# A four-layer graph network kernel: first-layer normalisation moved between engines, one widening step moved a head earlier, and more filler products at the end of the load

## The reference

```python
h = jnp.maximum(_layernorm(x, axis=-1), 0.0)
x = x + _L0_gnn_ref(h, adj, L0_gnn_weight, L0_gnn_bias)    # D^-1/2 adj^T D^-1/2 (h @ W0) + b0
h = jnp.maximum(_layernorm(x, axis=-1), 0.0)
x = x + _L1_gnn_ref(h, adj)                                # (adj + mask/norm) @ h, over its row sums
h = jnp.maximum(_layernorm(x, axis=-1), 0.0)
x = x + _L2_gnn_ref(h, adj, L2_gnn_W, L2_gnn_a)            # 4 heads of attention, softmax(leaky(s_i+d_j)+adj)
h = jnp.maximum(_layernorm(x, axis=-1), 0.0)
x = x + _L3_gnn_ref(h, adj, L3_gnn_weight)                 # relu(adj @ (binary(h) @ sign(W3)^T))
```

## Time and profile before

| what | value |
|---|---|
| median of 3 runs | 707.07 us (706.51 to 708.0) |
| the profiled execution | 707.33 us, span of its instructions 705.5 us |
| TensorE busy | 684.2 us, 97% of the span |
| VectorE busy | 620.8 us, 88% |
| ScalarE busy | 459.4 us, 65% |
| GpSimd busy | 111.5 us, 16% |
| mean granted TensorE clock | 0.995 |

### The profile page before, as it was taken

One profiled execution on the slowest core, in us unless ns is written; L12 is line 12 of the kernel. 1 busy time (PEld: TensorE's weight loads), 2 busy tenths in 40 slices (PEclk: granted clock), 3 DMA queues, 4 the chain that ended last, 5 costly groups with the idle time before them and its releaser, 6 DMA issues.

```text
span 705.5 us, 15958 instructions
## 1 busy us (share of the span) xinstructions
PE 684.2 (97%) x6413; PEld 584.9 (83%) x6413; DVE 620.8 (88%) x1148; ACT 459.4 (65%) x798; POOL 111.5 (16%) x146
## 2 busy tenths in 40 slices
PE   3989999999999999999999999999999899999998
PEld 3876888888888974488888888888888788888887
DVE  7888999958898968899999999999999799994672
ACT  3987057638888328975559676587866678655650
POOL 3005722321123210011100021100211000000000
PEclk9998999999999999999999999999999999999999
DMA  9996999993799977779988799988999894464391
GB/s 334 378 336 258 424 426 308 303 230 123 219 271 252 208 189 191 192 180 246 214 189 248 143 222 249 232 236 175 203 235 239 222 199 78 83 191 139 130 311 38
DMA packets 169016, 159.53 MB, mean 226 GB/s; under 512 B 115760, under 2 KB 128752, under 8 KB 164720
## 3 DMA queue, kind: packets, MB, share of 16 engines
q1 hardware_dynamic: 147584, 100.32, 52.8%
q0 software_dynamic: 19056, 41.42, 26.2%
q10 hardware_dynamic: 2304, 16.78, 5.7%
HBM read 69.86 MB, written 52.46 MB: 173 GB/s over the span
## 4 chain that ended last, share of the span: by engine, by line
PE 88%; DVE 4%; ACT 4%; issue 3%; POOL 0%; ACTq 0%; POOLq 0%
PE ps L839 16%; PE ps L841 16%; PE ps L840 16%; PE ps L777 6%; PE ps L885 4%; PE ps L886 4%; PE ps L675 3%; PE ps L677 3%; PE ps L676 3%; PE ps L724 3%; PE ps L726 3%; PE ps L725 3%; DVE arena L1253 2%; PE ps L704 2%; DVE arena L1339 1%
## 5 line engine op out<-in xcount | busy, mean ns | idle before, releaser
L839 PE MATMUL ps<-arena 128*128 128x257 f16 x1024 | 279.9, 273 | 1.9 <-DVE arena L1477 1.9
L841 PE MATMUL ps<-arena 128*128 128x257 f16 x1024 | 279.4, 273 | 0.0
L840 PE MATMUL ps<-arena 128*128 128x257 f16 x1024 | 279.2, 273 | 0.0
L1169 ACT ACTIVATE arena<-arena 128x512 f16<-128x512 f32 x252 | 158.4, 628 | 98.0 <-PE ps L841 77.6
L1470 DVE SCALAR_TENSOR_TENSOR arena<-arena,w_j 128x512 f32<-128x512 f32 x256 | 190.0, 743 | 0.0
L1477 DVE TENSOR_TENSOR arena<-arena 128x512 f16<-128x512 f32 x256 | 175.7, 687 | 9.6 <-ACT arena L1169 9.3
L839 PEld LDWEIGHTS ps<-arena 128*128 128x128 f16 x1024 | 99.9, 98 | 14.8 <-ACT arena L1169 2.1
L840 PEld LDWEIGHTS ps<-arena 128*128 128x128 f16 x1024 | 100.3, 98 | 12.6
L841 PEld LDWEIGHTS ps<-arena 128*128 128x128 f16 x1024 | 99.8, 97 | 13.0
L724 PE MATMUL ps<-arena 128*128 128x257 f16 x256 | 70.3, 275 | 0.0
L726 PE MATMUL ps<-arena 128*128 128x257 f16 x256 | 69.7, 272 | 0.0
(11 more groups left out here) (149 smaller groups left out, 1068.0 us busy)
## 6 DMA issues: line engine op xcount, KB each, us to landing
adj_t<-arena POOLq DMA_DIRECT2D x32, 1024.0 KB, 7.9
arena<-in_adj_dram SPq DMA_DIRECT2D x32, 512.0 KB, 6.2
arena<-in_adj_dram SPq DMA_DIRECT2D x16, 1024.0 KB, 6.1
adj_parts<-arena ACTq DMA_DIRECT2D x16, 1024.0 KB, 22.1
arena<-adj_t SPq DMA_DIRECT2D x64, 256.0 KB, 4.9
arena<-adj_t SPq DMA_DIRECT2D x10, 1024.0 KB, 6.7
x<-arena POOLq DMA_DIRECT2D x15, 512.0 KB, 6.2
arena<-u_rows SPq DMA_DIRECT2D x4, 1024.0 KB, 14.7
```

The source lines that it names most:

```text
L839: mm(ps[:, bank, 0:DE], hi, ht_hi[:, head, j, 0:DE], start=s, stop=False)
L840: mm(ps[:, bank, 0:DE], hi, ht_lo[:, head, j, 0:DE], start=False, stop=False)
L841: ins = mm(ps[:, bank, 0:DE], lo, ht_hi[:, head, j, 0:DE], start=False, stop=e)
L1169: nc.scalar.activation(p_hi[:, j % 4, :], prob[:, j % 4, :], copy).then_inc(p_hi_done, 1)
```

## The change

Three things change.

1. The normalised blocks of block 0 go straight into `hw[t]`, each to its own place, instead of into two buffers in turn. VectorE normalises only blocks 0, 4, 8 and 12, at halves 0, 4, 8 and 14 (`NORM_AFTER`). GpSimd normalises the other twelve, three after each of its roots.
2. `WIDEN_AFTER`: block 12 is widened after group 6 (was 7), 13 after 7 (was 8), 14 and 15 after 8 (were 8 and 9).
3. `unread`: three products instead of one per half for n = 24 to 30, and eight instead of six after the last half.

```diff
-        h0_n = view(160 * KB, [2, D], F32)
+        NORM_AFTER = (0, 4, 8, 14)
-        WIDEN_AFTER = {0: (6,), 1: (7,), 3: (8,), 4: (9, 10), 5: (11,), 7: (12,), 8: (13, 14), 9: (15,)}
+        WIDEN_AFTER = {0: (6,), 1: (7,), 3: (8,), 4: (9, 10), 5: (11,), 6: (12,), 7: (13,), 8: (14, 15)}
...
+                pool.wait_ge(rstd_done, p + 1)
+                for t in range(XP * p + 1, XP * p + XP):
+                    nc.gpsimd.tensor_scalar(hw[:, t, :], x[:, t, :], mean_var[:, t, 0:1], rstd[:, t:t + 1],
+                                            ALU.subtract, ALU.mult).then_inc(pool_normed, 1)
...
             def h0_transposes(t):
-                pe.wait_ge(normed, t + 1)
+                if t % XP == 0:
+                    pe.wait_ge(normed, t // XP + 1)
+                else:
+                    pe.wait_ge(pool_normed, t // XP * (XP - 1) + t % XP)
...
-                                              h0_n[:, t % 2, c * P:(c + 1) * P],
+                                              hw[:, t, c * P:(c + 1) * P],
...
-                    unread(1)
+                    unread(1 if n < row_slot(NB - 1) + 2 else 3)
             ins.then_inc(deg_done, 1)
-            unread(6)
+            unread(8)
...
             def h0_norm(t):
-                if t % XP == 0:
-                    dve.wait_ge(rstd_done, t // XP + 1)
-                if t >= 2:
-                    dve.wait_ge(h0_t_ps, t - 1)
-                v.tensor_scalar(h0_n[:, t % 2, :], x[:, t, :], mean_var[:, t, 0:1], rstd[:, t:t + 1],
+                dve.wait_ge(rstd_done, t // XP + 1)
+                v.tensor_scalar(hw[:, t, :], x[:, t, :], mean_var[:, t, 0:1], rstd[:, t:t + 1],
...
-                for t in range(NB):
-                    if row_slot(t) - 1 == n:
-                        h0_norm(t)
+                if n in NORM_AFTER:
+                    h0_norm(XP * NORM_AFTER.index(n))
```

More of the change, by code:

```diff
@@ L254, in gnn_stack @@
         normed = sem("normed")
+        pool_normed = sem("pool_normed")
         h0_t_done = sem("h0_t_done")
```

## The result

| what | before | changed |
|---|---|---|
| median | 707.25 us (706.51 to 708.0, 4 runs) | 713.06 us (711.26 to 714.42, 4 runs) |
| ratio | | 1.0081, 95% interval 1.0056 to 1.0106 |
| the profiled execution | 707.33 us, span 705.5 | 714.42 us, span 712.6 |
| first product of block 0 | 63.73 us | 67.03 us |
| group 0's addition to x (start of block 2's queue) | 329.27 us | 336.36 us |

The changed kernel is 5.8 us slower, where 3 us less was forecast. The traces differ by 7.1 us in span. 3.3 us of it arise in the load, 3.8 us between 67 us and group 0's addition, and nothing net in block 2 and after. A trace is of one execution, and some lie far from the median of their kernel (unread_only's is of 707.89 us, its median 710.52; swap_extra's 710.61 and 706.90; mended's 712.72 and 707.75; tiny_128's 711.84 and 708.09).

A forecast was written before the change was run, and what follows sets the result against it. TensorE, busy 97% of the span, was taken as the bound, leaving only its gaps. Load 1.0, unread products 0.1 and widening 1.86 sum to 2.96 us less: median 704.1 us, 8-in-10 range 702.5 to 706.3.

The forecast's parts named there:

- a GpSimd round is 5.6 us, blocks come in time: Load: a 1.24 us root and three normalisations take 5.6 us, serving four blocks that TensorE takes in about 6 us.
- the hold: Load: time a GpSimd normalisation keeps VectorE from working, taken as 0.3 us, between 0.15 and 0.52.
- No normalisation waits for more than one `adj_low`: Load: GpSimd and VectorE take turns after each instruction, so a normalisation behind one `adj_low` takes 1.45 us in all.
- The third rival: Load: GpSimd holds VectorE 0.9 us per normalisation, rounds last 7.4 us, kernel slower at 709.5 us; chance 0.06.
- the first rival: Load: the hold is an addition's 0.52 us, so the load loses 0.5 us net, kernel at 705.6 us; chance 0.17.
- 2 us less work reach the end with 1.0 us: Load from 35 us to half 24: VectorE has six normalisations less, 2 us; 1.0 us (0.5 to 1.5) shortens the load.
- The clock: Load's tail: the extra unread products keep TensorE's granted clock at 1.0 from 56 to 64 us.
- the fit into a half: Load's tail: column sums and three unread products take TensorE 1.07 us per half against VectorE's 1.15, 0.08 to spare.
- The 0.1 us of gain: Load's end: eight unread products at full clock end at 63.0 instead of about 63.9 us, gaining 0.1 us.
- block 12's transposes landed by 479: Block 2's widening: GpSimd can take block 12 at 479 instead of 487.1 us, and `add_low` follows at 486.
- the bound of 0.6: Block 2's widening: group 7's addition, issued at 487 behind block 12's `add_low`, stalls TensorE at most 0.6 us; 0 expected.

The follow-up runs named there:

- unread_only: The kernel before with only the extra unread products (three per half from half 24, eight at the end): 710.52 us, ratio 1.0039.
- swap_extra: unread_only with 34 instead of 50 warm-up products ahead of the load: 706.90 us, ratio 0.9992 against the kernel before.
- mended: The changed kernel with GpSimd's four roots before its normalisations and 34 instead of 50 warm-up products: 707.75 us, ratio 1.0012 against the kernel before.
- tiny_128: The kernel before with 128 products more ahead of block 1, sixteen one-column ones per half at n = 24 to 30: 708.09 us, ratio 1.001.
- roots_first: The kernel before with twelve normalisations moved to GpSimd, which takes all four roots ahead of them: 707.31 us, ratio 1.001.
- unread_low3: unread_only with block 3's `add_low` behind the root of block 13 in GpSimd's queue: 708.37 us, ratio 1.0022 against the kernel before.
- no_norms: The changed kernel with all sixteen normalisations back on VectorE: 708.43 us, ratio 1.0017 against the kernel before.
- tiny_64: The kernel before with 64 products more ahead of block 1, eight one-column ones per half at n = 24 to 30: 709.08 us, ratio 1.0021.
- widen_only: The kernel before with only `WIDEN_AFTER` changed, blocks 12 to 15 widened earlier: 705.97 us, ratio 0.9984.

## Why the prediction was wrong

**Part 1, the step "a GpSimd round is 5.6 us, blocks come in time", failed.** The normalisation was priced as a short one-input instruction that waits behind one `adj_low` (1.45 us in all), from a cast of 128 columns in 0.29 us. It takes 1.22 us alone and 2.07 beside VectorE. The bounds of 0.15 to 0.52 us were bounds on the hold, and the duration itself had none. "No normalisation waits for more than one `adj_low`" fell too: the longest took 3.58 us, 2.4 more than alone. So rounds took 6.5 to 8.7 us instead of 5.6.

**The wait that the change adds was not priced.** The lists of the order, ahead of the prediction, show it: VectorE's normalisation now waits for a root, and the root stands behind three normalisations of the round before. The prediction asked when blocks reach TensorE and never what is queued ahead of the roots. With its own 5.6 us a round this would have cost nothing: the second and third root would have been ready at about 19.2 and 24.8 us (an estimate: 12.3 + 5.6 + 1.24, and 5.6 more), and VectorE asked for them at 20.3 and 27.4 (21.27 - 0.93 and 29.49 - 2.12). It was the long rounds and the order together. roots_first keeps the long normalisations, takes only the order away, and the 3.9 us are gone but for 0.4.

**The hold was looked for on the wrong side.** From g_lo's 0.94 against 0.475 us it was concluded that GpSimd holds VectorE. Here `adj_low` grew by 0.026 us on average (1.247 against 1.221), 0.8 us in the whole load, and GpSimd's instruction by 0.85. By the rule that the prediction quotes from the Trainium skill (SBUF — State Buffer, SBUF: two separate sides), that each blocks the other for a whole instruction, an `adj_low` beside a 1.22 us normalisation should have been up to 1.2 us longer. The longest was 0.2 longer, so for VectorE the trace doesn't agree. The third rival had slower rounds (7.4 us) and 709.5, so its size and side were nearest, but by a mechanism (VectorE held for 0.9 us) that did not occur, so that was luck.

Two sums of this part were off as well. Up to 35 us VectorE saves six or seven normalisations, 2.0 to 2.3 us, and pays nine holds, 4.7 us at 0.52: that is some 2.5 us more, not 1.5, so the first rival was priced 1 us too low. And one of VectorE's own four normalisations lies behind 35 us (at 39.35), where the prediction counts none.

**"2 us less work reach the end with 1.0 us", failed.** VectorE had its twelve normalisations less, but the load ended no sooner even in roots_first (first product at 63.69 against 63.73). VectorE's gain turned into waiting for ScalarE.

**Part 2, a term that the sum left out.** The clock and the fit into a half were right (58 to 60 us at 1.00; 1.14 us a half). The 0.1 us of gain is too small to be seen: with part 2 the first product is at 62.91, 63.16 and 63.93 us (unread_only, unread_low3, no_norms), and at 63.10 to 63.73 in four traces whose load is that of the kernel before. That 16 more products ahead of everything move every later fetch of TensorE's program, and come with a loss of 3.3 us, was not in the profile as I read it.

**Part 3, mechanism right, its size in part luck.** The gap went in all five traces with the earlier widening. But 1.86 us was the figure of one execution. Of the 15 traces with the old widening 14 have the gap, with 0.4 to 2.3 us, and tiny_64 has none. Over all 15 the mean is 1.1 us, near the 1.25 that widen_only gained by the medians. The step "block 12's transposes landed by 479" failed in the changed kernel: GpSimd could take the block only at 488.29, 481.2 in the time of before. So group 7's addition was issued at 497.2, not 487, and cost 0.5 us, inside the bound of 0.6. In widen_only block 12 came at 478.14 and it cost nothing.

## What to carry to other kernels

When work moves to an idle engine, price its duration there with the same operation, shape and operand count or give it bounds of its own, and list what its queue already serves. A short result that others wait for belongs ahead of the long work, not between it. When a queue on an off-path engine has 0.3 us of slack ahead of a result on the path, as at block 1's root, any change elsewhere can spend it. Compare a change of a few microseconds also with the same number of idle instructions in its place, since the place in the program alone was worth 3 us here. And take a gap's price from several executions: the one of 1.86 us was anything from 0 to 2.3 in others.

## What the hardware showed that was not expected

- TensorE's program comes in by DMA, 51 packets of 16 KB of about 0.95 us. Block 9's `widen_high`, a 1 MB transfer of GpSimd's queue, landed after 9.0 to 9.2 us where a packet started 6.5 to 7.2 us behind its issue, and after 7.2 to 8.0 otherwise; block 4's showed no such difference. 16 products more ahead went with 3 us more, a whole packet of 128 with about 1 us or nothing. Why a packet of 0.95 us on one DMA engine should delay a landing by more than itself is not shown.
- A GpSimd subtract-and-multiply with two scalars per row takes 1.22 us for 128 by 256 float32 alone, and 2.07 us (up to 3.58) beside `adj_low`, which itself is lengthened by at most 0.2 us.
